# Negated maxima written into the slot of the maxima, and that slot stored and loaded whole for the scores

## The reference

```python
xn = layernorm(x)
# differential attention: 16 heads, each with two halves s of head width 8, B*H = 64 heads in all
q, k, v = split(xn @ w_qkv.T)
a_s = softmax(q_s @ k_s.T / sqrt(8)) @ v          # s = 1, 2; v is 16 wide
o = rms_norm(a_1 - lam * a_2) * w * (1 - 0.2);  y1 = o @ w_proj.T + b_proj
# mixture of experts: 8 experts, top 2 of each token, capacity 1024 rows, hidden width 1024
y2 = g1 * eo[slot1] + g2 * eo[slot2];  eo = gelu(rows @ w_gate[e]) @ w_down[e]
out = x + y1 + y2
```

## Time and profile before

| | us |
|---|---|
| median of 3 executions (lowest, highest) | 1757.05 (1755.74, 1757.13) |
| the profiled execution, own time | 1760.05 |
| its span, first to last instruction | 1758.1 |
| experts, first to last chunk's start | 125 to 586 |
| attention, first to last exponential | 618 to 1724 |

### The profile page before, as it was taken

The page is one execution under the profiler, slowest core; times in us unless marked ns, Lnnn a source line. Parts: engine busy times, 40 slices in busy tenths (PEclk is TensorE's granted clock), DMA queues, the critical chain, the costliest instruction groups (busy, mean ns, idle before and its releaser), DMA issues.

```text
span 1758.1 us, 77503 instructions
## 1 busy us (share of the span) xinstructions
PE 1651.2 (94%) x33602; PEld 905.0 (51%) x33603; DVE 1489.7 (85%) x2450; ACT 1289.9 (73%) x2509; POOL 759.8 (43%) x1233
## 2 busy tenths in 40 slices
PE   6998999999999989999999999899799999999989
PEld 5556666666676634444444444444344444444437
DVE  7878787878888789999998998899699999989816
ACT  4463344343534289999999999899789999989884
POOL 0126656566666213433343243334633433633253
PEclk9989999999999999999999999999999999999999
DMA  8653331321231042222222222222222122222103
GB/s 264 215 192 119 105 113 52 108 96 56 92 93 55 22 144 61 60 63 62 59 61 66 58 58 64 57 63 57 58 62 60 58 64 57 61 61 62 53 23 103
DMA packets 120853, 142.27 MB, mean 81 GB/s; under 512 B 25152, under 2 KB 83136, under 8 KB 120512
## 3 DMA queue, kind: packets, MB, share of 16 engines
q1 hardware_dynamic: 114368, 120.54, 22.6%
q0 software_dynamic: 6144, 16.79, 3.3%
HBM read 102.92 MB, written 34.34 MB: 78 GB/s over the span
## 4 chain that ended last, share of the span: by engine, by line
PE 55%; ACT 17%; DVE 10%; issue 7%; SPq 4%; POOL 3%; DMA 3%; ACTq 0%; POOLq 0%; DVEq 0%
ACT arena_t L928 17%; PE banks L1418 13%; PE banks L1433 13%; PE banks L1469 9%; PE banks L1447 6%; SPq L479 4%; PE banks L1389 3%; PE banks L1449 3%; DVE row_half L1145 3%; DVE row_half L1136 3%; PE banks L1404 2%; PE banks L1284 2%; DMA qk_ring<-k_stack 1%; PE banks L1548 1%; DVE rest L1021 1%
## 5 line engine op out<-in xcount | busy, mean ns | idle before, releaser
L928 ACT ACTIVATE arena_t<-banks 128x512 f32<-128x512 f32 x2048 | 1016.4, 660 | 103.8 <-PE banks L1418 102.6
L1145 DVE TENSOR_REDUCE row_half<-banks 128x1 f32<-128x512 f32 x1472 | 914.6, 680 | 79.2 <-PE banks L1404 75.2
L1418 PE MATMUL banks<-arena_q 50*32 50x512 bf16 x8192 | 749.9, 384 | 29.1 <-ACT arena_t L928 9.2
L1433 PE MATMUL banks<-arena_t,v_ring 64*17 64x256 f32 x16384 | 708.1, 379 | 7.2 <-DVE o_turned_sb L1215 5.3
L1404 PE MATMUL banks<-qk_ring 48*32 48x512 bf16 x5888 | 576.0, 385 | 29.5 <-DMA qk_ring<-k_stack 11.3
L1418 PEld LDWEIGHTS banks<-arena_q 50*32 50x32 bf16 x8192 | 222.3, 90 | 498.0 <-ACT arena_t L928 360.9
L1136 DVE TENSOR_REDUCE row_half<-banks 128x2 f32<-128x1024 f32 x288 | 334.3, 1219 | 18.8 <-PE banks L1389 17.0
L1433 PEld LDWEIGHTS banks<-arena_t,v_ring 64*17 64x17 f32 x16384 | 293.9, 93 | 86.6 <-issue 18.3
L909 ACT ACTIVATE arena_t<-banks 128x512 f32<-128x512 f32 x128 | 76.4, 597 | 275.5 <-PE banks L1469 269.4
L777 POOL TENSOR_TENSOR hidden_parts<-arena_t,hidden_parts 128x512 fp32r<-128x512 f32 x128 | 164.6, 1289 | 152.8 <-ACT hidden_parts L911 149.8
L671 POOL TENSOR_TENSOR inv_sum<-inv_sum,half_factor 128x16 f32<-128x16 f32 x64 | 13.9, 218 | 471.1 <-DVE inv_sum L1219 471.1
(11 more groups left out here) (140 smaller groups left out, 1192.9 us busy)
## 6 DMA issues: line engine op xcount, KB each, us to landing
v_ring<-v_heads SPq DMA_DIRECT2D x128, 68.0 KB, 2.7
expert_rows<-arena_r SPq DMA_DIRECT2D x16, 512.0 KB, 3.0
q_stack<-arena_q SPq DMA_DIRECT2D x8, 768.0 KB, 3.8
k_stack<-arena_q SPq DMA_DIRECT2D x8, 768.0 KB, 4.0
qk_ring<-q_stack SPq DMA_DIRECT2D x128, 48.0 KB
qk_ring<-k_stack SPq DMA_DIRECT2D x128, 48.0 KB
arena_q<-q_stack SPq DMA_DIRECT2D x128, 48.0 KB
arena_q<-k_stack SPq DMA_DIRECT2D x128, 48.0 KB
```

The costliest lines, as they stand in the source:

```text
L928: nc.scalar.activation(probs[:, kg % PSLOTS, qh, :], banks[:, st_bank(STEPS * g + i), :], ACT.Exp).then_inc(exp_done, 1)
L1145: nc.vector.tensor_reduce(row_half[:, g % 2, h, u:u + 1], banks[:, half_bank(n), :], AX.X, ALU.max, negate=True).then_inc(half_done, 1)
L1418: mm = pe.matmul(banks[column:column + QUAD, st_bank(STEPS * g + i), :], score_qk[g % SCORE_SLOTS][rows, 1, KEYS * kg + QUAD * c:KEYS * kg ...
L1433: mm = pe.matmul(o_columns()[QUAD * c:QUAD * c + VP, s, :], v_ring[rows, g % SLOTS, kg % 2, kg // 2, :], probs[rows, kg % PSLOTS, c // 2, ...
```

## The change

- `MAX_SLOTS` goes from 3 to 4.
- The slots of the maxima are filled with ones once, by POOL at the start (4 memsets). The memsets of the score slots go.
- The turned negated maxima are not stored to DRAM but copied by DMA into rows 48 and 49 of each half of the head's slot of the maxima, plane 0 (`neg_rows_in`: 8 DMAs for the first 18 heads, 4 for the others). The slot, 114 partitions of 4 KB, is then stored to DRAM in one DMA (`store_full`), and the score slot is loaded from there in one (`load_for_scores`).
- The load of a slot of the maxima waits for the store of the head that had the slot.
- In attention the turn is 30 steps after the join rather than 16 (16 for the last four heads), the store comes at the start of the next step of SP, and the fourth group of the roots is at head 62 rather than 61.
- In experts the pairs of places 10 and 11 change from (4, 6) to (6, 4), and the down product waits for 11 reductions rather than 12. SP's order in a chunk: maxima loads, score loads, v, negated rows in, the wait for the chunk's end, rows, weights, full store.

```diff
 INVERT_AT = 7
-MAX_SLOTS = 3
+MAX_SLOTS = 4
 SCORE_SLOTS = 3
 EARLY = 2 * 8 * EARLY_HEADS
...
 HEAD_DMAS = 2 * 2 * len(RUNS)
-NEG_DMAS = 4
...
 SROWS = STACK + NEG
+FULL = HALF + SROWS
...
 def build_program(nc, x, w_qkv_t, w_proj_t, b_proj, lambdas, norm_w, wg, w_gate, w_down, out):
...
         k_stack = nc.dram_tensor("k_stack", (NPART, G, 2, HD, N), BF16, kind="Internal").ap()
-        neg_store = nc.dram_tensor("neg_store", (G, 2, NEG, N), BF16, kind="Internal").ap()
+        full_stack = nc.dram_tensor("full_stack", (G, FULL, 2, N), BF16, kind="Internal").ap()
         v_heads = nc.dram_tensor("v_heads", (G, P, TB, VP), F32, kind="Internal").ap()
         token_rows = nc.dram_tensor("token_rows", (T, D), F32, kind="Internal").ap()
...
         HALF_BANKS = (2, 3, 4)
-        EXPERT_SMAX_PAIRS = 4 * (2, 4, 6) + 2 * (0, 4, 2)
+        EXPERT_SMAX_PAIRS = 3 * (2, 4, 6) + (2, 6, 4) + 2 * (0, 4, 2)
         OT_BANK = 5
         DOWN_BANK = 6
...
         ones_set = sem("ones_set")
-        neg_out = [sem(f"neg_out{i}") for i in range(2)]
-        neg_in = [sem(f"neg_in{i}") for i in range(SCORE_SLOTS)]
+        neg_in = [sem(f"neg_in{i}") for i in range(MAX_SLOTS)]
+        full_out = [sem(f"full_out{i}") for i in range(MAX_SLOTS)]
         smax_psum = sem("smax_psum")
         half_psum = sem("half_psum")
...
         ROOT_HEADS = ((0, H), (H, 2 * H), (2 * H, 3 * H), (3 * H, G - 4), (G - 4, G))
-        ROOT_AT = (35, 37, 51, 61)
+        ROOT_AT = (35, 37, 51, 62)
         ROOT_LAST_AT = 16
         ROOT_STEPS = 13
...
         def neg_turn_step(h):
-            return join_step(h) + STEPS // 2
+            return join_step(h) + (30 if h < G - 4 else 16)
...
             return STEPS * (g + 1) + INVERT_AT
...
-        def max_load_chunk(h):
-            return (2 * TB * (h - MAX_SLOTS) + 2 * TB - 1) // BETWEEN + 1
-        def max_load_step(h):
-            return STEPS * (join_step(h - MAX_SLOTS) // STEPS + 1)
-        def neg_load_step(h):
-            return max(h - SCORE_SLOTS + 1, neg_turn_step(h) // STEPS if h in late_heads else 0)
-        def neg_stored(h):
-            return 16 * NEG_DMAS * (h // 2 + 1)
+        def store_step(h):
+            return neg_turn_step(h) // STEPS + 1
+        def score_load_step(h):
+            return max(h - SCORE_SLOTS + 1, store_step(h) if h in late_heads else 0)
+        def neg_landed(h):
+            return 16 * sum(8 if k < EARLY_HEADS else 4 for k in range(h % MAX_SLOTS, h + 1, MAX_SLOTS))
+        def full_landed(h):
+            return 16 * (h // MAX_SLOTS + 1)
...
                 k = g % MAX_SLOTS
-                if MAX_SLOTS <= g < MAX_SLOTS + EARLY_HEADS:
-                    sp.wait_ge(smax_psum, 2 * TB * (g - MAX_SLOTS + 1))
-                elif g >= MAX_SLOTS + EARLY_HEADS:
-                    sp.wait_ge(half_psum, STEPS * (g - MAX_SLOTS - EARLY_HEADS + 1))
+                if g < MAX_SLOTS:
+                    sp.wait_ge(ones_set, g + 1)
+                else:
+                    sp.wait_ge(full_out[k], full_landed(g - MAX_SLOTS))
                 for s in range(2):
                         load_plane(max_qk[k], max_in[k], g, s, plane)
...
                 k = g % SCORE_SLOTS
-                if g < SCORE_SLOTS:
-                    sp.wait_ge(ones_set, g + 1)
-                else:
+                sp.wait_ge(full_out[g % MAX_SLOTS], full_landed(g))
+                if g >= SCORE_SLOTS:
                     sp.wait_ge(st_psum, STEPS * (g - SCORE_SLOTS + 1))
-                for s in range(2):
-                    for plane in range(2):
-                        load_plane(score_qk[k], score_in[k], g, s, plane)
+                sp.dma_start(score_qk[k][0:FULL], full_stack[g]).then_inc(score_in[k], 16)
...
-            def store_neg(g):
+            def neg_rows_in(g):
+                k = g % MAX_SLOTS
                 sp.wait_ge(neg_turned, g + 1)
-                for b in range(P // QUAD):
-                    if g < EARLY_HEADS:
-                        rows = neg_store[g].rearrange("s a (t b i) -> b (s a t) i", b=P // QUAD, i=QUAD)[b]
-                    else:
-                        rows = neg_store[g, 1 - b // 2].rearrange("a (u b i) -> b (a u) i", b=2, i=QUAD)[b % 2]
-                    sp.dma_start(rows, neg_blocks[QUAD * b:QUAD * (b + 1), g % 2, :]).then_inc(neg_out[g % 2], 16)
-            def load_neg(g):
-                k = g % SCORE_SLOTS
-                sp.wait_ge(neg_out[g % 2], neg_stored(g))
-                if g >= SCORE_SLOTS:
-                    sp.wait_ge(st_psum, STEPS * (g - SCORE_SLOTS + 1))
-                for s in range(2):
-                    sp.dma_start(score_qk[k][HALF * s + STACK:HALF * s + SROWS, 0, :], neg_store[g, s]).then_inc(neg_in[k], 16)
+                if g < EARLY_HEADS:
+                    for s in range(2):
+                        rows = max_qk[k][HALF * s + STACK:HALF * s + SROWS, 0, :].rearrange("r (t b i) -> r t b i", b=P // QUAD, i=QUAD)
+                        for b in range(P // QUAD):
+                            first = QUAD * b + NEG * TB * s
+                            sp.dma_start(rows[:, :, b, :], neg_blocks[first:first + NEG * TB, g % 2, :]).then_inc(neg_in[k], 16)
+                else:
+                    for b in range(P // QUAD):
+                        first = HALF * (1 - b // 2) + STACK
+                        rows = max_qk[k][first:first + NEG, 0, :].rearrange("r (u b i) -> r u b i", b=2, i=QUAD)
+                        sp.dma_start(rows[:, :, b % 2, :], neg_blocks[QUAD * b:QUAD * (b + 1), g % 2, :]).then_inc(neg_in[k], 16)
+            def store_full(g):
+                k = g % MAX_SLOTS
+                sp.wait_ge(neg_in[k], neg_landed(g))
+                sp.dma_start(full_stack[g], max_qk[k][0:FULL]).then_inc(full_out[k], 16)
...
                 sp.dma_start(w_ring[s][:, 1, LO].rearrange("p (f d) -> p f d", f=FC), w_down[bass.ds(e, 1)].rearrange("e (k p) d -> p (e k) d", p=P)).then_inc(down_in[s], 16)
...
                     if n == HEAD_AT:
+                        sp.wait_ge(ones_set, 1)
                         for s in (0, 2):
                     if HEAD_AT <= n < HEAD_AT + 4:
...
                     load_for_max(n + 1)
-                for h in range(MAX_SLOTS, EARLY_HEADS + MAX_SLOTS):
-                    if max_load_chunk(h) == n:
-                        load_for_max(h)
-                if 2 <= n < 2 + SCORE_SLOTS:
-                    load_for_scores(n - 2)
+                for h in range(late_heads.start):
+                    if join_chunk(h) + 1 == n:
+                        load_for_max(h + MAX_SLOTS)
                 for h in range(SCORE_SLOTS):
-                    if join_chunk(h) + 1 == n:
-                        load_neg(h)
+                    if join_chunk(h) + 2 == n:
+                        load_for_scores(h)
                 if n < SLOTS:
                     load_v(n)
+                for h in range(late_heads.start):
+                    if join_chunk(h) == n:
+                        neg_rows_in(h)
                 sp.wait_ge(down_copied, 4 * n + 4)
                 if s == 1 and e + 2 < E:
...
                     if join_chunk(h) == n:
-                        store_neg(h)
+                        store_full(h)
...
                 expert_step(n)
...
             def attention_step(g):
-                for h in range(EARLY_HEADS, EARLY_HEADS + MAX_SLOTS):
-                    if g == 0 and max_load_chunk(h) >= 2 * E:
-                        load_for_max(h)
-                if 1 <= g <= G - SCORE_SLOTS:
-                    load_for_scores(g - 1 + SCORE_SLOTS)
+                for h in late_heads:
+                    if store_step(h) == g:
+                        store_full(h)
+                for h in range(late_heads.start):
+                    if g == 0 and join_chunk(h) + 1 >= 2 * E:
+                        load_for_max(h + MAX_SLOTS)
+                for h in range(SCORE_SLOTS, G):
+                    if score_load_step(h) == g:
+                        load_for_scores(h)
                 if 1 <= g <= G - SLOTS:
                     load_v(g - 1 + SLOTS)
-                for h in range(EARLY_HEADS + MAX_SLOTS, G):
-                    if max_load_step(h) == STEPS * g:
-                        load_for_max(h)
+                for h in late_heads:
+                    if store_step(h) == g and h + MAX_SLOTS < G:
+                        load_for_max(h + MAX_SLOTS)
                 for h in late_heads:
                     if neg_turn_step(h) // STEPS == g:
-                        store_neg(h)
-                for h in range(SCORE_SLOTS, G):
-                    if neg_load_step(h) == g:
-                        load_neg(h)
+                        neg_rows_in(h)
...
                 attention_step(g)
...
+            for k in range(MAX_SLOTS):
+                nc.gpsimd.memset(max_qk[k], 1.0).then_inc(ones_set, 1)
...
             def find_rows(n):
                 s = n % 2
...
             pool.wait_ge(qk_psum, 4 * B)
```

(9 more changed lines are left out.)

## The result

| | us |
|---|---|
| before, median of 4 executions | 1757.09 |
| after, median of 4 executions (lowest, highest) | 1688.03 (1684.39, 1695.48) |
| ratio of after to before | 0.9612, 95% interval 0.9593 to 0.9632 |
| after, the profiled execution, own time | 1684.39 |
| its span | 1682.6 |

The forecast was 1712 with a range of 1699 to 1732: the direction was right, the size was not. The gain is 69 us in place of 45.

The account below looks back on a forecast made before the run. Bound: near-full PE, ACT and DVE in quiet heads, plus SP's full issuing, set by DMA number; experts PE-bound. From the profiled 1760.05 us, attention 32 and experts 13 off gave 1715, or 1712 against the median; range 1699 to 1732.

Parts of the forecast that it names:

- the quiet pace: Attention: 16.63 us per head in a quiet stretch, so 64 heads need 1064 of the stage's 1106 us.
- part 1: Attention: storing and loading the slot once relieves SP; late landings and neg_store waits go, 15.0 us.
- head 20: Start of attention: stored in step 1, used from 2.21, so less cover than other heads, 10 us.
- the cover of 22 us: Attention: slack between a head's turned rows being stored and reloaded and their earliest use, 1.3 heads.
- Head 10: Experts, chunk 8: its load waits for head 6's store behind two weight loads; cost 0, at worst 3 us once.
- Part 2: Attention: later turn cuts the stall at head 38, gain 7.3 us; later root eases the last turn, gain 5.
- Part 3: Experts: new bank order closes the 0.71 us gap before line 1447; net 0.6 us in 15 chunks, 9 us.
- wait of 0.15 us at place 10: Experts: pair 6 is reused two places apart instead of three, so this tile can wait up to 0.15 us.
- B: Attention: SP and the DMAs held the quiet pace; a quarter of 0.8 us per head comes, 1700 us; chance 0.10.
- A: Attention: landings stay late though SP is relieved, so the 15.0 us stay; 1729 us; chance 0.12.
- C: Experts: the bank-order wait only moves and the turn's stall stays; 1728 us; chance 0.08.
- D: Attention: SP stands at the turned maxima, cover is used up, every late head waits; 1804 us; chance 0.04.

Follow-up runs that it names:

- the unused slot: Kernel before with qk_ring allocated one slot deeper and that slot never used, so only addresses behind it move: 1757.41 us, ratio 0.9985.
- part 1 alone: Kernel before with only the slot stored and loaded whole and four slots; old turn, roots and bank order kept: 1750.16 us, ratio 0.9960.
- the three edits: Changed kernel with 128-row slot store and load, 4 MB load behind first maxima load, second root at step 39: 1713.04 us; with an unused tile 1669.84.
- part 3 alone: Kernel before with only the expert bank pairs at places 10 and 11 exchanged and the down product's wait at 11: 1745.22 us, ratio 0.9904.

## Why the prediction was right or wrong

**What bounds the kernel.** That SP's issuing is full and that the number of DMAs matters was right (a quarter of the bytes gives nothing, no score loads give 70 us, twelve more DMAs per head cost 240 us over the changed kernel). The step that failed is the price of attention: "at the quiet pace 64 heads would need 64 x 16.63 = 1064 us", the pace taken as the kernel's own, and on top of it part 1 priced at the 15.0 us of PE's waits. Without the stops the pace is 15.7, with ACT busy throughout, though SP be as full as before (the unused slot), and part 1 is worth 44 to 46 us; with SP relieved and the stops there the pace stays at 16.2 to 17 (part 1 alone). That SP's sum came out at 16.6 us, "exactly the head's time", was a coincidence with the stops; SP's limit shows in the mean of 17.2 us. The signs stood in the same rows: ACT was busy 252.63 of 266.00, DVE 249.66, PE 257.74. None of three engines was full, and I read "all three are near full" as a bound. An engine that is the bound has no idle time in a quiet stretch. And chance had its part in the miss: the profile that was read had the stops, and that of the changed kernel had not. Had both had them, the same prediction would by the estimate above have met 1721 us, 9 over its forecast and inside its range, with the same error in its step.

**Part 1.** The late landings went nearly as forecast: 15.0 us in the waits of before, 5.5 in the changed kernel. Mis-sized was what this is worth: 44 to 46 us where nothing else stops PE, since the wait rows show 15 us of late data while SP's lateness was hidden behind the stops (without the stops the same two waits of the kernel before, but for the unused slot, are 40.5 us); 8 us where the stops stay. The sum held neither. Issuing cost 0.27 and 0.26 us in place of 0.6. I allowed 3.8 us for the landing, and 4 us of moving alone is more than that; elsewhere than at head 20 the cover of 22 us took it. The exception is head 20. I had it used from step 2.21, with a cover of 10 us; by the kernel's own formulas its first use is 2.69, and head 21 turns at 6.28 and head 25 is used from 9.34, not 6.09 and 9.11 (the 3.34 heads counted from step 6 are right). So the cover of head 20 was some 18 us, and still it did not do, as I had left out what stands ahead of its load in SP's queue at the start of attention, 16 short DMAs of 10.63 us among it. Then the store took 6.06 us and the last of the load's twelve DMAs 6.47 to land, where I had allowed 3.8 and 3.15 (SP's timeline, then the chain that ended last):

```profile
617.59 10.63 SPq L514 DMA_DIRECT2D qk_ring<-neg_blocks  x16
...
640.38 1.84 SPq L479 DMA_DIRECT2D qk_ring<-k_stack  x3
```

```profile
628.26 6.06 DMA full_stack<-qk_ring
...
641.79 6.47 DMA qk_ring<-k_stack
```

PE stood for it:

```profile
648.30 0.61 PE L1409 MATMUL banks<-qk_ring 48*32 48x512 bf16 x4 [5.12 <-DMA qk_ring<-k_stack]
```

It is the longest wait of PE in attention that the change leaves. In the three edits head 2, in which it falls, takes 16.6 in place of 23.5 us, but head 1 takes 21.6 in place of 16.4, so that most of it moved. Head 10, where I feared 3 us, cost nothing: the ninth chunk is 28.95 us.

**Part 2.** Right. DVE's wait at head 38 was forecast at 3.4 us and the last turn's was to be harmless; the timeline of DVE in the changed kernel answers to the earlier trace rows:

```profile
1233.51 0.21 DVE L1168 STREAM_TRANSPOSE neg_blocks<-neg_parts 128x32 bf16<-128x32 bf16 x1 [3.79 <-POOL neg_parts L777]
```

PE's share of it is 3.1 us (3 forecast) and the 4.9 us at line 1433 are gone. The part was put at 7.3 + 5 = 12.3 us and measured 13.1 behind part 1, though only 7 on the kernel before, where SP is the limit behind it.

**Part 3.** The mechanism was right, the size was off: 0.6 us a chunk forecast, 29.94 - 28.95 = 1.0 measured, some 15 us in all in place of 9, as part 3 alone (14) and behind part 1 (15.1) also show. The term was the gap of 0.71 us before line 1447. The windows had no better number: PE idle 89.83 - 87.79 = 2.04 us in three chunks is 0.68 by its modelled ends, and the chunk shrank by 1.0; the wait's price has to be read from the pace of the chunks on both sides, not from the idle time of an engine whose ends are modelled. The feared wait of 0.15 us at place 10 did not come. In the ninth chunk 4.5 us went, of which 3.5 are left beside part 3, as forecast with 3.3 for the store ahead of the weights; the granted clock rose there from 0.95 to 1.00 as well, and the two were not told apart.

**The rivals.** B's number came, its mechanism did not. I gave it 0.10 and priced it at a quarter of the 0.8 us per head; nearly all of the 0.8 came. But what held the quiet pace was not SP, it was the stops, and that the profile of after is free of them is nothing that the change is shown to do. The argument against B, "PE showed no wait for it in those heads", looked only for waits with a name: the 24 waits on "issue" were in the same list. A is wrong (the late landings went, but for head 20), C is wrong (both gains came in full). D did not come; the kernel with twelve more DMAs is the nearest thing to it.

The 69 us are thus 44 to 46 of part 1 where nothing stops PE and 23 of parts 2 and 3; up to 2 may be the absence of the stops by itself, which the unused slot doesn't tell from nothing. On a chip with the stops the change would by the estimate come to about 1721 us.

## What to carry to other kernels

Before a quiet stretch is called the pace of a kernel, find the engine with no idle time in it; if there is none, something unnamed holds it, and rows that end in "issue" by the dozen belong to it. Where two limits lie on top of each other, single edits give nothing and their sum is not the whole: test each with the other away. Note on which chip each profile was taken, and compare traces of the same chip before a difference is put down to an edit: a median of the kernel before that agrees on all chips does not show that it spends its time in the same way on them. And give a large DMA a slowest dimension of 128.
